# Gated cross-attention and experts: three engine programs joined into one, a last accumulation in banks of its own, counts placed later

## The reference, cut to what is computed

```python
def layer(x, ctx):                       # x: 4096 rows of 512; ctx: 3202 rows of 512
    e = layernorm(x)
    Sim = (e @ w1)[:, None] + (ctx @ w2)[None, :] + (e * w3) @ ctx.T + b_sim
    hq = softmax(Sim, axis=1) @ ctx                    # a row for each row of x
    hc = softmax(Sim.max(axis=1)) @ e                  # one row for all
    feats = concatenate([e, hq, e * hq, e * hc])       # 2048 wide
    x = x + tanh(g_xattn) * (feats @ W_qv + b_qv)
    h = layernorm(x)
    gates = softmax(h @ w_router + b_router)           # 8 experts, the best 2
    # an expert takes the first 640 rows that chose it, others are dropped
    y = weighted sum over a row's experts of gelu(h @ w1[e] + b1[e]) @ w2[e] + b2[e]
    return x + tanh(g_ffn) * y
```

## Time and profile before

| | us |
|---|---|
| median of 3 runs | 2373.12 |
| lowest, highest | 2372.64, 2373.97 |
| the profiled execution | 2374.48 |
| its span, first to last instruction | 2372.70 |
| attention, merge and route, experts | 0 to 1193, 1194 to 1519, 1520 to 2373 |
| PE busy | 94% |

### The profile page before, as it was taken

One profiled execution on the slowest core, in us unless ns is written; L12 is line 12 of the kernel. 1 busy time (PEld: TensorE's weight loads), 2 busy tenths in 40 slices (PEclk: granted clock), 3 DMA queues, 4 the chain that ended last, 5 costly groups with the idle time before them and its releaser, 6 DMA issues. The chain is left out here.

```text
span 2372.7 us, 46798 instructions
## 1 busy us (share of the span) xinstructions
PE 2227.0 (94%) x16737; PEld 1607.9 (68%) x16737; DVE 1632.3 (69%) x3440; ACT 1134.9 (48%) x1602; POOL 146.7 (6%) x143
## 2 busy tenths in 40 slices
PE   3899999999999999999879999499999999999998
PEld 2788888888888888888634444265564656556563
DVE  5788888888888888886946668456464555646450
ACT  4565555545555555454623334254463635446360
POOL 0000000000000000000012112101011010101101
PEclk9999999999999999999989999699999999999999
DMA  9901110011111001102255443333334353333421
GB/s 234 265 28 46 44 45 21 24 45 45 45 44 45 27 18 45 45 27 96 92 197 195 185 170 143 110 98 89 102 89 111 136 133 98 93 102 89 109 81 22
DMA packets 175435, 215.41 MB, mean 91 GB/s; under 512 B 116580, under 2 KB 116708, under 8 KB 167132
## 3 DMA queue, kind: packets, MB, share of 16 engines
q1 hardware_dynamic: 164444, 193.75, 25.1%
q0 software_dynamic: 10880, 20.52, 4.4%
HBM read 123.66 MB, written 71.52 MB: 82 GB/s over the span
## 5 line engine op out<-in xcount | busy, mean ns | idle before, releaser
L1248 PE MATMUL ps<-arena 128*128 128x256 f16 x4800 | 560.0, 276 | 58.7 <-DMA arena<-arena 48.6
L1266 PE MATMUL ps<-arena 128*128 (+1 forms) x4864 | 560.5, 273 | 9.9 <-DVE arena L820 8.0
L1248 PEld LDWEIGHTS ps<-arena 128*128 128x128 f16 x4800 | 472.7, 99 | 125.0 <-issue 39.9
L1266 PEld LDWEIGHTS ps<-arena 128*128 128x128 f16 x4864 | 475.1, 98 | 70.2 <-issue 9.5
L1894 PE MATMUL ps<-arena 128*128 128x320 f16 x3072 | 421.2, 300 | 23.2 <-DMA arena<-rows 23.2
L1909 PE MATMUL ps<-arena 128*128 128x512 f16 x1920 | 415.7, 379 | 0.0
L1894 PEld LDWEIGHTS ps<-arena 128*128 128x128 f16 x3072 | 301.6, 98 | 142.6 <-issue 23.3
L1909 PEld LDWEIGHTS ps<-arena 128*128 128x128 f16 x1920 | 187.9, 98 | 225.3
L1124 ACT ACTIVATE arena<-ps,arena (+1 forms) x192 | 148.8, 775 | 293.5 <-PE ps L1248 293.5
L1643 PE MATMUL ps<-arena 128*128 128x512 f16 x1080 | 248.8, 389 | 6.4 <-PEq L444 4.3
L1816 DVE SCALAR_TENSOR_TENSOR arena<-arena 128x640 f16<-128x640 f32 x128 | 113.1, 883 | 131.7 <-ACT arena L1861 131.7
(11 more groups left out here) (241 smaller groups left out, 1796.1 us busy)
## 6 DMA issues: line engine op xcount, KB each, us to landing
arena<-in_L_ffn_w SPq DMA_DIRECT2D x64, 1024.0 KB, 10.5
arena<-feats SPq DMA_DIRECT2D x16, 1536.0 KB
arena<-in_x SPq DMA_DIRECT2D x32, 512.0 KB, 3.9
feats<-arena SPq DMA_DIRECT2D x16, 1024.0 KB, 3.9
rows<-arena SPq DMA_DIRECT2D x1, 10320.0 KB, 31.3
feats<-arena SPq DMA_DIRECT2D x16, 512.0 KB, 3.5
out<-arena SPq DMA_DIRECT2D x16, 512.0 KB, 2.8
arena<-in_L_xattn_W_qv SPq DMA_DIRECT2D x4, 1024.0 KB, 9.7
```

The source lines that it names most:

```text
L1248: mm = pe.matmul(out, ctxT[:, 2 * t + h, s, k, :], query[:, r, k, :], start=(k == 0 and s + r == 0), stop=(k == KD - 1 and s == 1))
L1266: mm = pe.matmul(psA[:, k, :], ctxN[:, 2 * t + h, s, k * P:(k + 1) * P], prob[:, bass.ds(a % 3, 1), r, h, :].rearrange("p o i -> p (o i)") ...
```

## The change

1. **One program for each engine.** The three functions open no block; each returns its five engine programs, and `gated_layer` puts them one behind the other in a single block. The ends of attention and of merge_and_route go, with drains and barriers. In their place PE waits on `acc_step` at the end of attention, POOL waits for the last low part on `feats` (`mg.f_lo`), and SP waits, ahead of the first expert's row load, until all 32 row sets have been sent (`sent[v]`).
2. **Last accumulation.** Iteration 16 accumulates into banks 0, 1, 7 and 6 (`psA_last`) with its sums in bank 4; its matmuls run with k outermost (`products_last`), and only those of k = 3 wait for DVE's reciprocal on the old bank. `take_acc` of the block before moves behind the first `low_and_sum`. Block 0's merge goes to banks 2 and 3 (`psY_first`).
3. **Weights of the merge.** `mg.scales` and the division of hc move to t = 8; the four folds are spread over t = 9 to 12 (`fold_part`).
4. **Start of the merge stage.** DVE and ACT wait for less of POOL's constants; `y_part` adds its bias ahead of the wait for the product.
5. **Counts and route_2.** `counts(b-1)` at the end of PE's body b becomes `counts(b-2)` between the two groups of 18 matmuls of half 0. `route_2(b-1)` at the end of DVE's body becomes `route_2(b-2)` at the start of the next. What is left over, `counts(14)` and `route_2(14)`, stands behind the loop.
6. **Splits.** The first expert's eight weight parts are split three, three and two at a time in bodies 12, 13 and 14, none in body 15.

The core of the diff, without regard to indentation:

```diff
@@ attention
-            if not first:
+            if not first and not last:
                 take_acc(b - 2)
...
                 low_and_sum(a0, 0)
+            if last:
+                take_acc(b - 2)
...
-                        if t == 9:
+                    if t == 8:
                             mg.scales(dve)
-                        if t == 10:
                             mg.fold_hc(dve)
+                    if t >= 9:
+                        mg.fold_part(dve, t - 9)
...
+        def products_last(b, t):
+
+            a = (b - 1) * NP + t
+            pe.wait_ge(p_ready, a + 1)
+            for k in range(KD):
+                if t == 0 and k == KD - 1:
+                    pe.wait_ge(acc_step, ACK * (b - 2) + 1)
+                for h in range(2):
+                    mm = products_of(a, t, h, k, psA_last)
+            mm.then_inc(av_done, 1)
...
-            sums(NB - 1)
+        sums(NB - 1, psL_last)
             for q in range(QT):
-                mg.merge(pe, q, psS_first)
+            mg.merge(pe, q, psY_first)
+        pe.wait_ge(acc_step, ACK * NB)
@@ merge_and_route
+    SPLITS = {2: (0, 1, 2), 3: (3, 4, 5), 4: (6, 7)}
...
-    with ExitStack() as st:
...
-        block = st.enter_context(nc.Block())
...
+    def gpsimd(pool):
+        pool.wait_ge(mg.f_lo, mg.f_all)
...
-            dve.wait_ge(made, 5)
...
+            if routed == 2:
+                route_2(b - 2, v, n - 1)
+            y_part(b, v, 0, not routed)
                 if routed:
                     route_1(b - 1)
+            y_part(b, v, 1, not routed)
                 norm_part(b, v, n)
-                if routed:
-                    route_2(b - 1, 1 - v, n if v else n - 1)
...
-            act.wait_ge(made, 5)
+        act.wait_ge(made, 1)
...
                 merge(b, v, 0, 0, old)
+            if old:
+                counts(b - 2)
                 merge(b, v, 0, 1, old)
...
                 merge(b, v, 1, 1, old)
-                counts(b - 1)
...
+        counts(NB - 2)
             turn_rows(NB - 1, 1)
@@ experts
+        for v in range(2):
+            sp.wait_ge(sent[v], 16 * rows_sent)
             turn_rows(0)
@@ gated_layer
+        block = st.enter_context(nc.Block())
+
+        @block.sync
+        def _(sp):
+            sp_1(sp)
+            sp_2(sp)
+            sp_3(sp)
```

More of the change, by code:

```diff
@@ L1046, in _ @@
-                if t == 11:
-                    tail_low()
-                    common_scale()
-            running_max(0, NP - 1)
-            tail_columns(1)
-            merge_maxima(0)
-            maxima(0)
-            iteration(1, first=True)
-            with dve.Fori(2, NB - 1) as b:
-                iteration(b)
-            iteration(NB - 1, norms=False)
-            iteration(NB, last=True, norms=False)
-            for k in range(FT):
-                mg.low(dve, k)
-            take_acc(NB - 1)
@@ new lines, in vector @@
+        running_max(0, NP - 1)
+        tail_columns(1)
+        merge_maxima(0)
+        maxima(0)
+        iteration(1, first=True)
+        with dve.Fori(2, NB - 1) as b:
+            iteration(b)
+        iteration(NB - 1, norms=False)
+        iteration(NB, last=True, norms=False)
+        for k in range(FT):
+            mg.low(dve, k)
+        take_acc(NB - 1, psA_last, psL_last)
+        mg.factors(dve)
+        for k in range(KD):
+            products(NB - 1, k)
+            lows(NB - 1, k)
@@ L1224, in _ @@
-            scores(0, NP - 1)
-            iteration(1, first=True)
-            with act.Fori(2, NB - 1) as b:
-                iteration(b)
-            iteration(NB - 1, norms=False)
-            iteration(NB, last=True, norms=False)
-            for k in range(FT):
-                mg.high(act, k, mg.steps)
-                if k == 2:
-                    mg.gates(act)
-            for k in range(KD):
-                high_hq(NB - 1, k)
-                high_eh(NB - 1, k)
-        @block.tensor
@@ L1334, in merge_and_route @@
-def merge_and_route(nc, ps, arena, cst, x, feats, rows, x1_out, mg, ew):
+                    probabilities(a0 + t + 2, t + 2)
+                if not first and t < KD:
+                    high_hq(b - 2, t)
+                    high_eh(b - 2, t)
+                if norms:
+                    if t == 1:
+                        norm_sd(b + 1)
+                    if t == 3:
+                        norm_hi(b + 1)
+                    if t in (9, 12):
+                        query_hi(b + 1, (t - 9) // 3, True)
@@ new lines, in iteration @@
+                if not last and t + AHEAD < NP:
+                    scores(b, t + AHEAD)
+                if not last and t == 12:
+                    keep_maxima(b)
+                if first and t < 7:
+                    for u in range(2 * t, min(2 * t + 2, NP)):
+                        squares(u)
+                if last and 4 <= t < 8:
+                    mg.sum_part(act, t - 4)
+        act.sem_inc(scores_ready, 2)
+        act.wait_ge(made, 2)
+        act.activation(warm, zero, ACT.Sqrt, bias=lneps[:, 0:1], scale=1.0)
@@ new lines, in sem @@
+    def sem(name):
+        return st.enter_context(nc.semaphore(name))
+    made, start = sem("made2"), sem("start")
+    f_loaded, x_loaded = mg.f_loaded, mg.x_loaded
+    x_stored = [sem("x1_stored_0"), sem("x1_stored_1")]
+    y_done = mg.y_done
+    y_step, sd_done, hi_done, turned, xt_ready, logits, e_done, r_step, counted = (sem(s) for s in (
+        "y_step", "sd_done", "row_hi", "turned", "xt_ready", "logits", "e_done", "r_step",
+        "counted"))
+    sent, row_free = [[sem(f"{name}_{v}") for v in range(2)] for name in ("sent", "row_free")]
@@ L1694, in experts, with tail @@
-def experts(nc, ps, arena, cst, ew, b2, rows, out):
+            act.wait_ge(y_step, YK * b + 4 * QT)
+            act.activation(sd, mv[:, :, 1], ACT.Sqrt, bias=lneps[:, 0:1], scale=1 / LN_SCALE ** 2)\
+               .then_inc(sd_done, 1)
+            act.wait_ge(row_free[v], n + 1)
+            for q in range(QT):
+                act.wait_ge(y_step, YK * b + 4 * QT + 2 + q)
+                act.copy(halves[v][:, q, 0:D], xn[:, q, :]).then_inc(hi_done, 1)
+        def tail(c):
+            for q in range(QT):
+                act.wait_ge(turned, QT * c + q + 1)
+                act.copy(xT[:, q].rearrange("p s k i -> p (s k) i"), psR[q]).then_inc(xt_ready, 1)
+            act.wait_ge(r_step, RK * c + 3)
+            act.activation(ex, lg, ACT.Exp).then_inc(e_done, 1)
@@ L1696, in experts @@
+    return sync, gpsimd, vector, scalar, tensor, sent
+def experts(nc, st, ps, arena, cst, ew, b2, rows, out, sent, rows_sent):
     E, D, F, KD, KF, CH, SK = ew.E, ew.D, ew.F, ew.KD, ew.KF, ew.CH, ew.SK
```

2369 lines of the change are left out of this document (1177 added, 1192 removed).

## The result

The changed kernel takes 2345.74 us (2344.76 to 2346.45, four runs) against 2373.55 for the kernel before, a ratio of 0.9877 with a 95% interval from 0.9861 to 0.9894: 27.8 us less. The forecast was 2339.4 with a range from 2330 to 2364. The profiled execution has a span of 2343.8 us, against 2372.7.

What follows compares the result with a forecast made beforehand. PE, busy 94% of the span, was taken as the bound, its idle time to be cut. Gains 0.5 + 6.6 + 20.9 + 0 + 5.7 = 33.7 us gave a median of 2339.4, range 2330 to 2364.

Steps and rivals of the forecast that it cites:

- The loop: Merge bodies 2 to 15: 242.9 us against 263.8, a gain of 20.9, as PE stops waiting at the counts.
- held to 16.0: Loop, one body: router ends at 13.3 after body start, sends hold its signal to 16.0, mask ready at 19.1.
- nothing is held: Loop, following body: first send at 12.4, close to router's end at 13.3, so no delay; mask ready at 16.5.
- the sign that the forecast had named: Changed profile's loop: DVE's "remote" waits on the router in every second body, with bodies of 17.1 us.
- The rival with a ring of 19.2 us: Loop: router's result held until 5.7 after first send in every body; 22 us come back, 2361 to 2362; chance 0.18.
- The first seam: Attention to merge: store queues behind 4 MB, body 2 starts 8.4 us earlier, less 1.8 for the clock: 6.6.
- The second seam: Merge and route to experts: SP's first row load goes out at 1514.0 instead of 1519.67, a gain of 5.7.
- the last block: End of merge, where two splits no longer stand ahead of the router result: gain 0, from -1.5 to 1.5.
- The last iteration: End of attention: DVE limits it, only its idle time can be saved; gain 0.5 us, from -0.5 to 0.9.
- Rival 2: Attention to merge: store not queued, lands at 1198.9, PE does not idle, 7.4 + 1.8 more saved: 2330; chance 0.09.
- Rival 5: Merge and experts loops: PE waits for code at 13 returns, 2.4 us each: 2371, or 2404 if dearer; chance 0.03.
- Rivals 3 and 4: Half the hold or about 1 us lost a body: 2350, chance 0.07; both seams give nothing: 2352, chance 0.03.

Runs made afterwards that it cites:

- the two experiments on the counts: Kernel before with only counts and route_2 placed later: 2354.4 us; changed kernel with both back in their old places: 2366.2 us.
- the last version: Changed kernel plus a POOL drain behind the last send and the four 1 MB expert-weight loads issued singly behind blocks 4 to 7: 2330.7 us.
- the one with the drain alone: Changed kernel plus one POOL drain behind its last send: 2342.8 us.

## Why the prediction was right, point by point

**The loop** was the largest term, 20.9, and it came as 20.4; the two experiments on the counts, 18.8 and 20.5, lie on either side of it. The 0.5 is in the bodies with splits, for which the forecast had 3.5 us and the trace has 4.1. Its reasoning was right in the cause (sends delay the router's signal, DVE's mask comes late, PE stands at the counts) and wrong in one step: that the signal is "held to 16.0" in one body and "nothing is held" in the next. The wait is not for 5.7 us behind the first send in one body and none in the next. Over the whole merge stage there are still seven "remote" waits,

```profile
DVE arena L1522 <- remote: 21.7, 7, 3.8
```

and in a regular body POOL's first send and DVE's read of the router are

```profile
1300.52 0.97 POOL L1475 DMA_INDIRECT rows<-arena  x1 [11.52 <-DVE arena L1573]
```

```profile
1304.07 0.23 DVE L1522 SCALAR_TENSOR_TENSOR arena<-ps,arena 128x16 f32<-128x16 f32 x1 [2.96 <-remote]
```

3.6 us apart, and nearly alike in bodies 6 to 9. The router ends 1.9 behind the first send, DVE reads 1.7 later, so the mask is ready some 5 us after the router and some 3 us ahead of the counts. The delay shrank with the distance and did not alternate, against the sign that the forecast had named ("remote" waits in every second body). PE's time was the same, because both readings stay below the 7.6 us that the counts now have behind the router's end: that the time came out right in spite of the step is due to a margin of some 3 us, and in that sense to luck. The rival with a ring of 19.2 us needed the old delay to persist, and it did not.

**The first seam** was right in kind and short in size. The store did wait for the 4 MB, block 2 did come 7 to 8 us earlier and not 15.8. Two terms were too kind by 1 us each. The store landed at 1209.7, forecast 1209.9, but block 2's load was issued 0.5 later and took 7.4 and not 6.5. The low clock cost 2.9 on 18 matmuls (6.95 in place of 4.04), not 1.8. The rows that I had named for it give 6.10 - 3.97 = 2.1, and they are from a stretch in which only part of the matmuls ran at the lower level: the granted clock was 0.66 from 1214.3 to 1220.4 in the kernel before, and 0.57 in the first 6.9 us of body 2 in the changed one.

**The second seam** gave 5.7 exactly, but the step "5.7, from 5 to 6" left out where that time would return. POOL's drain is not a fixed cost of a block's end that vanishes with it: its length goes with the indirect DMAs behind it, and the one drain that is left has them all. This is the one effect that the forecast put at nothing, 2.8 us, the largest part of the miss of 4.7 in the profiled execution. The rest is the two terms above, the 0.5 of the loop and 1.0 from the start of attention, less 1.5 in the last block and the experts. The 1.0 stays open. It is not due to the new last iteration (the same point lies at 1127.7 with the old one). But in all six profiles of the joined program that point lies at 1127.5 to 1129.5, and in all four with three blocks at 1126.6 to 1127.1, so that joining may have cost a microsecond or two in the first stage; no run here isolates it.

**The last iteration** was right: 0.6 in place of 0.5, by DVE's idle time and not by PE's. **Rival 2** (store not queued) fell: 12.6 us. **Rival 5** (waits for code at the returns) fell too: PE's list has no such wait, and the experts' matmuls end as far behind their start as before, within 0.6. No run shows the 5 us that this rival had for a fetch behind a block load; DVE's waits of 2.4 us at twelve loop starts are in both kernels. **Rivals 3 and 4** fell with bodies of 17.09 us and with seams that gave 4.5 and 5.7.

## What to carry to other kernels

On an engine that works in order, put a wait behind work that is ready: two small matmuls at a body's end cost some 19 us over 14 bodies here, and next to nothing a quarter of a body later. A large background load should not stand in a queue ahead of a small transfer whose landing gates the next load; cut it into pieces and issue each behind the transfer that matters (here 12.1 us, the last version against the one with the drain alone). When a barrier is taken out, look where its work goes: what a drain had to wait for is still there at the next drain, and here a drain placed beside a load of 7 us cost nothing.

## What the runs showed of the hardware

POOL's drain took 0.50 us at the end of attention, where it had issued no indirect DMA, 2.68 us behind 32 of them, 3.33 behind 40, 5.29 behind 64 and 6.11 behind 104: about 0.083 us for each up to 64, and less for those beyond. POOL had waited for the landing of all of them before it drained (in the kernel before the last add landed at 2368.99 and the drain ran from 2369.17 to 2372.50), so the drain's time isn't that of the data. What POOL does in it stays open.

A matmul's signal reached DVE up to 2.8 us late while POOL's indirect sends were under way, and within 0.3 with half as many or with none at that time. DVE read 0.8 to 1.1 us behind the fourth send's end in nine bodies of the kernel before, and within 0.1 us of the third's end in five bodies of the changed one. Four sends of 1.06 MB together went with such a delay, and so did four of 0.55 MB in body 11 of the kernel before; with four of 0.23 MB and less, in bodies 13 to 15, it was 0.2 us at most. What exactly holds the signal stays open.
